# Products of zeros ahead of the first Gram matrix, one clearing moved on GpSimd, one square root moved on ScalarE

## The reference, cut to what matters

```
x = x + attn(layernorm(x), queries)
x = x + ffn(layernorm(x), ln1, ln2, wqkv, wo, gate_w, w13, w2)

attn(h, queries):                    # no softmax
    q = h @ queries.T
    return (q @ h.T) @ h             # per batch, 1024 x 1024 scores

ffn(x, ...):
    h = rmsnorm(x, ln1); qkv = h @ wqkv.T          # 16 heads of 8, 4 key/value heads
    rotate q and k; causal softmax attention; x = x + attn @ wo.T
    h = rmsnorm(x, ln2); softmax over 8 experts, top 2, renormalised
    out = sum over experts of silu(h w1.T) * (h w3.T) @ w2.T * weight
    return x + out
```

## Time and profile before

| what | us |
|---|---|
| median of 3 runs | 436.49 (436.24 to 441.15) |
| the profiled execution, its own time | 436.67 |
| its span in the profile | 434.9 |
| TensorE busy | 409.3 (94%) |
| VectorE busy | 343.0 (79%) |
| ScalarE busy | 287.7 (66%) |
| GpSimd busy | 215.5 (50%) |

### The profile page before, as it was taken

The page is one execution under the profiler, slowest core; times in us unless marked ns, Lnnn a source line. Parts: engine busy times, 40 slices in busy tenths (PEclk is TensorE's granted clock), DMA queues, the critical chain, the costliest instruction groups (busy, mean ns, idle before and its releaser), DMA issues.

```text
span 434.9 us, 8846 instructions
## 1 busy us (share of the span) xinstructions
PE 409.3 (94%) x3010; PEld 254.8 (59%) x3010; DVE 343.0 (79%) x569; ACT 287.7 (66%) x577; POOL 215.5 (50%) x358
## 2 busy tenths in 40 slices
PE   1987997999999999999999999999999999999995
PEld 1945443545455454554545545458878877888883
DVE  6696688879889898898989976546668998787773
ACT  3445563778878688786877969765774555555552
POOL 6000555435247364473644034135783886676673
PEclk9999967599999999999999999899999999999998
DMA  7905202001601020110200000012221422422300
GB/s 209 325 16 169 54 5 56 2 3 34 205 25 38 2 59 2 32 29 4 57 1 5 2 3 3 1 64 87 57 61 37 90 52 73 96 60 61 96 1 26
DMA packets 16983, 23.92 MB, mean 55 GB/s; under 512 B 2622, under 2 KB 7614, under 8 KB 16942
## 3 DMA queue, kind: packets, MB, share of 16 engines
q1 hardware_dynamic: 15982, 22.21, 18.3%
q0 software_dynamic: 960, 1.18, 1.1%
HBM read 18.08 MB, written 5.05 MB: 53 GB/s over the span
## 4 chain that ended last, share of the span: by engine, by line
PE 68%; DVE 16%; issue 9%; ACT 4%; POOL 2%; DMA 1%; POOLq 0%; DVEq 0%; ACTq 0%
PE o_bank L1495 16%; PE tb L1478 11%; PE sp L1436 9%; PE tb L1627 6%; PE sp L1627 6%; DVE mx L1085 5%; PE o_bank L1603 4%; DVE mx L1083 3%; PE sp L1442 2%; PE sp L1456 2%; PE o_bank L1606 2%; ACT pt L889 2%; DVE sw L1283 2%; POOL gl L664 1%; DVE stats L980 1%
## 5 line engine op out<-in xcount | busy, mean ns | idle before, releaser
L889 ACT ACTIVATE pt<-tb 128x512 f32<-128x512 f32 (+2 forms) x310 | 153.5, 563 | 51.4 <-PE tb L1478 46.0
L1085 DVE TENSOR_REDUCE mx<-sp 128x2 f32<-128x1024 f32 (+1 forms) x128 | 143.3, 1155 | 20.8 <-PE sp L1442 11.0
L664 POOL TENSOR_TENSOR gl<-gg,gh 128x512 fp32r<-128x512 f32 x64 | 88.9, 1391 | 46.5 <-ACT gh L940 46.3
L1436 PE MATMUL sp<-k_stk,q_stk 62*128 62x512 f32 (+3 forms) x384 | 83.3, 429 | 4.4 <-DVE mx L1085 1.2
L1478 PE MATMUL tb<-q_stk,k_stk 64*128 64x512 f32 (+3 forms) x372 | 85.6, 414 | 1.0 <-ACT pt L889 0.7
L1495 PE MATMUL o_bank<-pt,v_all 128*32 128x512 f32 (+3 forms) x768 | 82.7, 513 | 0.1
L639 POOL TENSOR_TENSOR tick<-tick 128x1 f32<-128x1 f32 x96 | 18.6, 194 | 120.5 <-ACT pt L889 120.2
L1478 PEld LDWEIGHTS tb<-q_stk,k_stk 64*128 64x128 f32 x372 | 43.3, 193 | 50.3 <-ACT pt L889 40.4
L1283 DVE TENSOR_TENSOR sw<-silu,wbc 128x512 f32<-128x512 f32 x62 | 54.6, 880 | 21.0 <-ACT silu L951 20.7
L951 ACT ACTIVATE silu<-tb 128x512 f32<-128x512 f32 x64 | 38.1, 597 | 38.1 <-PE tb L1627 37.8
L1436 PEld LDWEIGHTS sp<-k_stk,q_stk 62*128 62x128 f32 x384 | 41.4, 196 | 27.2 <-DVE mx L1085 11.4
(11 more groups left out here) (221 smaller groups left out, 571.9 us busy)
## 6 DMA issues: line engine op xcount, KB each, us to landing
wbc<-g_scr SPq DMA_DIRECT2D x31, 256.0 KB, 3.3
w13r<-w_t SPq DMA_DIRECT2D x1, 2048.0 KB, 11.5
q_scr<-q_hi SPq DMA_DIRECT2D x8, 256.0 KB, 3.1
q_stk<-q_scr SPq DMA_DIRECT2D x20, 96.0 KB
x<-x_in SPq DMA_DIRECT2D x4, 256.0 KB, 3.8
q_scr<-q_lo SPq DMA_DIRECT2D x4, 256.0 KB, 3.4
result<-x SPq DMA_DIRECT2D x4, 256.0 KB, 2.4
k_stk<-k_scr SPq DMA_DIRECT2D x10, 96.0 KB
```

The lines of the kernel that those rows point to most:

```text
L664: pool.tensor_tensor(gl[m % 4][:, :], gg[m % NGG][:, :], gh[m % 4][:, :].bitcast(F), ALU.subtract).then_inc(d_lo, 1)
L889: act.activation(pt[:, p0:p0 + 2 * len(heads) - 1:2, 0:w], src, ACT.Exp).then_inc(e_done, 1)
L1085: dve.reduce_max(half[:, :, t, i % TC], src[:, :, 0:w], AX.X).then_inc(s_free, 1)
L1436: last = pe.matmul(dst[:, k, w * x:w * (x + 1)], q_stk[n % NQ][rows_[k], i // TC, pair, P * (i % TC):P * (i % TC + 1)], k_stk[n % NQ][rows ...
```

## The change

GpSimd gets a new first step: it clears a new buffer `zero_bf` (128 x 512, bf16), counted on a new semaphore `zeros`. TensorE starts with 22 products of that buffer with itself, each 512 columns wide, into `XA[1][0]`, a bank whose first real use (batch 1's Gram matrix) starts a new sum. It then waits for fourteen constants, not sixteen; the wait for all sixteen now stands ahead of the first softmax scores (`units`), and so ahead of the first use of `v_all`. GpSimd does not clear `v_all` until VectorE has the variances of both batches (`a_var` at 2). On ScalarE `root(1, 2)` and `copy_t(0, 0)` change places.

```diff
+N_ZEROS = 22
...
+        zero_bf = sb("zero_bf", [P, C2], BF)
...
-        pad = sem("pad")
+        pad, zeros = sem("pad"), sem("zeros")
...
         def _(pool):
+            pool.memset(zero_bf[:, :], 0.0).then_inc(zeros, 1)
             pool.memset(warm[:, :], 1.0).then_inc(cst, 1)
...
+            pool.wait_ge(a_var, 2)
             pool.memset(v_all[:, :, :, HD:HD + 1], 1.0).then_inc(cst, 1)
             pool.memset(v_all[:, :, :, HD + 1:32], 0.0).then_inc(cst, 1)
...
             root(0, 1)
             normalise(0, 0)
             copy_g(0)
+            copy_t(0, 0)
             root(1, 2)
-            copy_t(0, 0)
             copy_m(0)
...
         def _(pe):
-            pe.wait_ge(cst, N_CST)
+            pe.wait_ge(zeros, 1)
+            for _ in range(N_ZEROS):
+                pe.matmul(XA[1][0], zero_bf[:, 0:P], zero_bf[:, :], start=True, stop=True)
+            pe.wait_ge(cst, N_CST - 2)
...
                 if n == s == part == 0:
+                    pe.wait_ge(cst, N_CST)
                     pe.wait_ge(a_raw, 6)
                     pe.wait_ge(a_vs, B)
```

## The result

| | us |
|---|---|
| before, median of 20 runs | 436.47 (436.19 to 441.21) |
| after, median of 20 runs | 435.37 (431.63 to 436.86) |
| ratio after to before, with its 95% interval | 0.9936 (0.9908 to 0.9965) |
| before, mean of the same 20 runs | 437.55 |
| after, mean of the same 20 runs | 434.75 |

The kernel became faster by 0.6% in the ratio, by 1.1 us in the median and by 2.8 us in the mean. The interval of the ratio is 1.5 to 4.0 us. That the median and the mean differ is the subject of most of what follows. Two lines of the page of after say where to look: the clock line has its dips in other slices than before (the fourth is now one of them), and the span is shorter by 0.9 us only.

The account below looks back on a forecast made before the run. TensorE, busy nearly throughout the 434.9 us span, was taken as the bound; the profiled 436.67 less a 2.5 us earlier add gave 434.2, and 0.18 lower for the median 434.0 us, range 431.8 to 436.7.

Parts of the forecast that it names:

- rival 2: TensorE's clock falls back in the gap before the first Gram matrix, which takes 3.75 us: 435.5 us; chance 0.06.
- Rival 3: Moved clearing hits batch 1's line 999 fully, ending at 14.6 to 15.0; gain 1.4 to 1.8, 434.9 us; chance 0.10.
- Rival 6: The gain is absorbed later by something at a fixed time that was overlooked: 436.5 us; chance 0.05.
- Zero products: TensorE's start: 22 products from near 1.4 us, pitch halving as the clock rises, the last done between 8.2 and 9.1.
- Rival 1: Zeros do not lift the clock; first Gram matrix takes 3.75 us, ending 1.45 us later: 438.0 us; chance 0.04.
- GpSimd's clearing: Moved off batch 0's line 999, which ends at 8.6 instead of 9.51; batch 1's group held to 13.6, costing 0.2.
- The swap: ScalarE's second root one copy later runs at 11.7 without waiting; in its old place it pushes the copy about 0.4.
- The add: VectorE's first add of attention, the yardstick: 13.9 us (13.4 to 14.1) against 16.43, a gain of 2.5 us.
- three small delays: Before the add: casts on GpSimd holding line 999, late zeros, batch 1's group held by clearing; two probably occur.
- I carry the gain over whole: From the add onward VectorE paces the chain up to the projections, so the 2.5 us reaches the end.
- rivals 4 and 5: Clock dips fall otherwise: in favour, down to 429.5 us, chance 0.10; or against, 438.7 us, chance 0.10.
- My bounds for the price of the two dips of before: Dips at 56.25 to 63.08 and 69.91 to 86.97: without them at most 2.1 + 2.4 = 4.5 us to be had.

Follow-up runs that it names:

- a_again: The changed kernel run once more with no edit; mean 434.2 us over 12 runs (431.49 to 437.03).
- zeros_only: The changed kernel with the clearing of `v_all` and ScalarE's root back in their old places, zero products kept; mean 435.8 us, ratio to before 0.9965.
- no_swap: The changed kernel with ScalarE's second root back ahead of the transposed copy; mean 434.55 us.
- fill_head: The changed kernel plus three zero products behind each of two placements of queries for the second chunk; mean 433.8 us, before 437.9.
- fill_all: The changed kernel with the fillings at the first scores and from 64 to 75 us, plus four zero products ahead of the first softmax scores; mean 428.8 us.
- no_zeros: The changed kernel without the 22 zero products, the clearing of their buffer kept; mean 436.5 us, ratio to before 0.9994.
- b_again: The kernel before run once more with no edit; mean 437.2 us over 12 runs (435.99 to 438.84).
- fill_mid: The changed kernel plus zero products where TensorE waits for VectorE's maxima, 64 to 75 us; mean 429.8 us, ratio to before 0.9812.
- fill_both: The changed kernel with both fillings, at the first scores and from 64 to 75 us; mean 430.1 us over six runs.
- mid_alone: The kernel before plus only the 64 to 75 us filling and GpSimd's clearing of `zero_bf`; mean 434.7 us, before 437.8.

## Why the prediction was right, point by point

The forecast was 434.0 us with a range of 431.8 to 436.7; the median is 435.37, the mean 434.75. Both lie in the range, and outside the 433.4 to 434.4 that the forecast itself was given: the median shows a gain of 1.1 us and the mean one of 2.8, where 2.5 was forecast. The mechanism of the start held; that the median still fell into the range is owed to its width, which was taken for rivals 2, 3 and 6, and none of these occurred.

*Zero products.* Forecast: from 1.4 on, the last between 8.2 and 9.1. Measured: from 1.38, the last record ending at 8.14 in the profile of after, and at 8.82, 9.08 and 7.82 in a_again, zeros_only and no_swap (start and duration of the group). The clock rose sooner than the working assumed, which counted 3.7 or 5.7 us from the first product: in the profile of after the records of the zeros shorten from 634 to 379 ns near 4.8 us. Rival 1, zeros that do not lift the clock, is refuted by the Gram matrix at 2.02 us in each of these, and rival 2 too: the pause of 0.46 us in front of it left the pace alone.

*GpSimd's clearing.* Forecast 8.6 for the end of line 1003 of batch 0, measured 8.46. In batch 1 I expected it to be held to 13.6, and in the profile of after it ended at 13.66. One of its instructions took 875 ns, where the shortest took 328:

```profile
L1003 DVE TENSOR_SCALAR y<-x,mv,rstd x3: 328/685/875, 12.2 to 13.1; 128x128 f32<-128x128 f32 x3
```

This is not what the moved clearing does as a rule. In a_again the group was asked for 0.95 us after the clearing began, where in after it was 0.97, and it was not late:

```profile
11.77 1.35 POOL L568 MEMSET v_all<- 128x1472 f32 x1
...
12.72 1.11 DVE L1003 TENSOR_SCALAR y<-x,mv,rstd 128x128 f32<-128x128 f32 x4
```

The same holds for the four fillings on top of after, fill_head to fill_all. The first instruction of the group does wait in all of them: in these five profiles and in no_swap it ends 0.07 to 0.08 us behind the recorded end of the clearing. But where it is asked for 0.4 us before that end, the wait only stretches it from 340 to at most 478 ns, and the group takes its 1.11 us. In the profile of after it ended at 13.09, which is 0.49 behind. There GpSimd's small clearings behind the big one started at 12.54, 12.80 and 13.05, at the pace that they have in no_zeros, where VectorE idles (12.42, 12.69, 12.94); in fill_head they were slowed (12.59, 12.95, 13.31). By these starts GpSimd went first through small clearings too in the profile of after, and VectorE waited for them; that is inferred. Why it did so there and not in the others stays open, and the agreement of 13.66 with the forecast is in part luck: I took 0.90 us from the end of the clearing to the end of the group, as in batch 0 before, and it was 1.06 in after and 0.65 in no_swap.

The Trainium skill ("SBUF — State Buffer", Who interferes with whom) says that a VectorE instruction that uses two ports and a GpSimd instruction exclude each other for a whole instruction. The traces agree: 1495 ns before, 875 in after, 924 in no_swap, each ending behind the clearing. Rival 3, the whole clearing in front of batch 1, did not occur.

*The swap.* I counted it as part of a path of 13.4 against VectorE's 13.6, so as nearly nothing; no_swap puts it at 0.0 against fill_head.

*The add.* Forecast 13.9 (13.4 to 14.1), measured 13.58; gain 2.85 against 2.5. Of the three small delays two did not occur: the casts on GpSimd did not hold line 1003, and the zeros were early enough in this execution. The third, the late group of batch 1, cost 0.34 us instead of 0.2 in this execution (13.66 against 12.21 + 1.11 = 13.32), and nothing in five other profiles.

*"I carry the gain over whole."* This is the step whose size was off for a single execution, through rivals 4 and 5, to which I gave 0.20 together. The mean agrees with the step on average: 2.8 us in the first set of 20 runs each and 2.8 in the set of b_again and a_again (437.0 over 46 runs against 434.2). The intervals, 1.5 to 4.0 and 1.9 to 4.5 us, leave room for a microsecond either way. The median says less, since before most runs stand close together (14 of 20 within 436.1 to 436.9) with a few far above, while after they spread over 5 us. Rival 6, a gain absorbed at a fixed time, is refuted: what was lost in the profile of after was lost exactly where the clock dipped, and fill_head, without a dip there, keeps it.

How exactly, a table of the profiles shows. It cuts each span at the write of keys (K), the first copy of maxima (M1) and the second (M2), and sets the dips beside each piece (the one at the very end, which all have, is left out, and so is the one of 3.4 us near 278, which all have but fill_mid, fill_both and mid_alone):

| kernel | to K | K to M1, dip | M1 to M2, dip | M2 to end, dip after M2 or just before |
|---|---|---|---|---|
| before | 30.86 | 17.11, none | 20.80, 6.8 | 366.1, 17.1 |
| b_again | 30.77 | 18.62, 3.4 | 19.06, none | 365.9, 17.1 |
| after | 28.00 | 18.67, 3.4 | 20.05, 3.4 | 367.3, 20.5 |
| a_again | 28.18 | 19.84, 6.8 | 20.05, 3.4 | 367.2, 20.5 |
| no_swap | 27.71 | 18.33, 3.4 (31.8 to 35.2) | 19.06, none | 366.0, 17.1 |
| fill_head | 27.71 | 17.12, none | 19.04, none | 365.9, 17.1 |
| fill_mid | 27.40 | 19.73, 6.8 | 19.05, none | 362.5, none |
| fill_both | 27.40 | 17.11, none | 22.44, 10.2 | 362.9, none |
| fill_all | 27.62 | 17.15, none | 19.11, none | 363.8, none |
| mid_alone | 30.75 | 18.71, 3.4 | 20.29, 6.8 | 362.9, none |
| zeros_only | 29.02 | 19.67, 6.8 | 19.06, none | 365.9, 17.1 |
| no_zeros | 29.10 | 17.14, none | 20.29, 6.8 | 367.3, 20.5 |

The same piece with a dip of the same length takes the same time within 0.5 us in all twelve profiles (within 0.1 in most), whatever the start was. So start and dips add up, and the costs can be read off: about 1.5 and 2.7 us for 3.4 and 6.8 us at half clock (1.2 GHz) between K and M1; 1.0, 1.2 to 1.8 and 3.4 between M1 and M2, for 3.4, 6.8 and 10.2 us; 3.4 and 4.7 behind M2 for 17.1 and 20.5 us together with the dip near 278 that these executions also have. fill_all has the one near 278 alone and takes 363.8 there, so about 1.1 of it is that one. (The fillings' own products are part of that piece.) My bounds for the price of the two dips of before, 2.1 and 2.4 us from VectorE's busy time, against 1.75 and about 2.3 measured, were good.

What stays open: why the runs of before stand so close together. Its two profiles show one dip each before M2, at 56 in one and at 42 in the other, for a sum of 37.9 and 37.7 us from K to M2; after's show two each (38.7 and 39.9), no_swap's one at 32 to 35 (37.4) and fill_head's none (36.2). If before nearly always has one and after anything from none to two, the pattern is explained, but these profiles are too few to show that, and one speaks against it: mid_alone does before's work up to 62 us, and its profile shows both dips there, 39.0 us from K to M2.

## What to carry to other kernels

A clock that follows TensorE's work makes the time of one kernel a mixture: compare means over many executions, read the granted clock beside every time, and cut the spans at landmarks before saying that a gain was lost. Where TensorE waits and a bank is free, products of zeros in the wait are cheap and can be worth more than the wait itself: 22 at the start, with a clearing moved, gave 2.8 us, and 33 more in later waits another 5.7. A clearing on GpSimd can hold VectorE's instruction beside it (1495 ns for one before); moved, it may hold the next such group instead. Here it made that group late in two of the seven profiles that have both the zeros and the moved clearing (after and no_swap), and one profile is not enough to price it.

## What the runs showed of the hardware

- With the granted clock reading 1.00 in the records of the first microseconds, TensorE ran at its lower level all the same: 3.75 us for the first Gram matrix against 2.02 after products of zeros. In these profiles the clock line cannot be trusted before its first change; the lengths of the records can (421 ns for a product of the Gram matrix before, 275 ns after).
- Zeros count as work for the clock: 22 products of nothing but zeros were followed by a Gram matrix at full pace in every profile that has them.
- A TensorE whose records fill a stretch can still lose its clock. Between 49 and 53 us of fill_both it was busy 3.50 of 4.0 us, in good part with products 32 columns wide or of 62 rows, and the clock fell to 0.50 at 53.5. In fill_all, which has four full-width products more there, all six runs had a clock of 0.992 or more.
- A VectorE instruction that was asked for while GpSimd's clearing ran ended 0.07 to 0.08 us behind the clearing's recorded end in six profiles, 0.32 in before and 0.49 in after. What its group of four loses depends on how much of the clearing is left: with 0.4 us left it took the undisturbed 1.11 us in five profiles (in fill_head it was asked for at 12.26, the clearing is recorded from 11.29 to 12.65) and 1.45 in after; with 0.85 left it took 1.50 in no_swap.
